# A four-layer graph network on one Trainium2 core: in the third layer, both context halves and the scores in one block of matmuls, output tiles together, a fourth context operand, the next group's norm first

## What is computed

```python
q, k, v = proj(Wq, bq), proj(Wk, bk), proj(Wv, bv)       # (b, 8, 64, 64) each
scores = einsum('bhqd,bhkd->bhqk', q, k) * SCALE * (adj + adj)
ctx = einsum('bhqk,bhkd->bhqd', softmax(scores), v)      # then heads side by side
x = x + einsum('bse,fe->bsf', ctx, Wo) + bo
```

## Time and profile before

| | us |
|---|---|
| median of 3 runs | 2230.99 (2229.94 to 2233.07) |
| profiled execution, its own time | 2231.61 |
| its span, first to last instruction | 2229.8 |
| TensorE busy | 2209.3 (99%) |
| DVE busy | 1366.5 (61%) |
| ACT busy | 778.8 (35%) |
| POOL busy | 740.7 (33%) |

### The profile page before, as it was taken

One profiled execution on the slowest core, in us unless ns is written; L12 is line 12 of the kernel. 1 busy time (PEld: TensorE's weight loads), 2 busy tenths in 40 slices (PEclk: granted clock), 3 DMA queues, 4 the chain that ended last, 5 costly groups with the idle time before them and its releaser, 6 DMA issues.

```text
span 2229.8 us, 39209 instructions
## 1 busy us (share of the span) xinstructions
PE 2209.3 (99%) x15756; PEld 1759.4 (79%) x15756; DVE 1366.5 (61%) x2712; ACT 778.8 (35%) x1393; POOL 740.7 (33%) x926
## 2 busy tenths in 40 slices
PE   8999999999999999999999999999999999999999
PEld 5788888888888887888888888888877777777776
DVE  4576666666666676555556454556787575757552
ACT  3433333333323333333232333323444343434342
POOL 1443433334433423233332223333353131313130
PEclk9999999999999999999999999999999999999999
DMA  6333333333333244322332332333453323333321
GB/s 211 76 81 105 90 102 83 88 94 87 91 92 108 83 135 133 105 81 81 91 109 83 106 98 81 85 93 104 138 160 112 100 91 99 94 95 97 92 62 38
DMA packets 142006, 220.52 MB, mean 99 GB/s; under 512 B 33920, under 2 KB 40064, under 8 KB 141824
## 3 DMA queue, kind: packets, MB, share of 16 engines
q1 hardware_dynamic: 135680, 209.62, 32.5%
q10 hardware_dynamic: 6144, 8.40, 1.6%
HBM read 84.71 MB, written 50.37 MB: 61 GB/s over the span
## 4 chain that ended last, share of the span: by engine, by line
PE 97%; DVE 1%; DMA 1%; SPq 0%; issue 0%; POOL 0%; ACT 0%; DVEq 0%; ACTq 0%; POOLq 0%
PE bank L319 54%; PE bank L309 32%; PE bank L335 3%; PE bank L555 3%; PE bank L490 2%; PE bank L460 1%; PE bank L356 1%; PE bank L299 1%; DVE yt L935 1%; PE bank L541 0%; DMA wq<-in_L_gnn_Wq_w 0%; DMA mcolt<-in_nodemask_cols 0%; SPq L957 0%; DVE hs L632 0%; DVE x L788 0%
## 5 line engine op out<-in xcount | busy, mean ns | idle before, releaser
L319 PE MATMUL bank<-w_hi,h3T_hi 128*128 128x512 f32 x768 | 305.6, 398 | 0.0
L319 PE MATMUL bank<-w_lo,h3T_hi 128*128 128x512 f32 x768 | 299.4, 390 | 0.0
L319 PE MATMUL bank<-w_hi,h3T_lo 128*128 128x512 f32 x768 | 299.1, 389 | 0.0
L964 ACT ACTIVATE Z<-bank 64x512 f32<-64x512 f32 x256 | 152.0, 594 | 319.0 <-PE bank L319 246.7
L319 PEld LDWEIGHTS bank<-w_hi,h3T_hi 128*128 128x128 f32 x768 | 144.1, 188 | 55.1 <-issue 26.0
L978 ACT ACTIVATE hn<-x,stA 128x512 f32<-128x512 f32 x192 | 140.8, 805 | 108.3 <-POOL stA L1224 108.3
L319 PEld LDWEIGHTS bank<-w_hi,h3T_lo 128*128 128x128 f32 x768 | 144.2, 188 | 30.4
L319 PEld LDWEIGHTS bank<-w_lo,h3T_hi 128*128 128x128 f32 x768 | 144.2, 188 | 29.0
L1219 POOL TENSOR_SCALAR stA<-stA 128x4 f32<-128x4 f32 x48 | 12.6, 264 | 426.6 <-DVE stA L609 426.5
L632 DVE STREAM_TRANSPOSE hs<-hn 128x512 f32<-128x512 f32 x192 | 123.8, 688 | 38.7 <-ACT hn L978 38.7
L920 DVE TENSOR_TENSOR yt<-bank,bsumt 128x512 f32<-128x512 f32 x64 | 43.9, 685 | 162.9 <-PE bank L555 162.9
(11 more groups left out here) (201 smaller groups left out, 5894.2 us busy)
## 6 DMA issues: line engine op xcount, KB each, us to landing
hGA<-hs SPq DMA_DIRECT2D x760, 64.0 KB, 2.0
mid<-x SPq DMA_DIRECT2D x32, 1024.0 KB, 4.5
x<-mid SPq DMA_DIRECT2D x32, 1024.0 KB, 5.7
x<-in_x SPq DMA_DIRECT2D x16, 1024.0 KB, 6.3
hGB<-hs SPq DMA_DIRECT2D x256, 64.0 KB, 2.0
out<-x SPq DMA_DIRECT2D x15, 1024.0 KB, 4.6
PT<-hs SPq DMA_DIRECT2D x120, 64.0 KB, 2.0
PT<-hs ACTq DMA_DIRECT2D x120, 64.0 KB, 2.1
```

Of the source, the lines that this page charges most:

```text
L319: ins = eng.matmul(b[:], h[l][:, k, ts], W[r][:, k, :], start=(k == 0 and i == 0), stop=(last and k == 3 and i == 2))
L964: return eng.activation(dst, src, ACT.Copy)
```

## The change

In every turn from 1 to 15 TensorE does both halves of the context behind the k projection, with the scores right behind them, and then the output tiles in one row. ACT normalizes the next group's tiles between the evictions of q and k, and copies both context halves behind k. DVE takes statistics and transposes of the next group first, then both context halves, then all four masks and maxima (`l2_masked`), with the output additions between these and the sums (`l2_sums`). In turn 15 the products for layer 3, and then layer 3's transposes, stand in front of the context's lo parts. There are four context operands up to group 13 and three for the last two (`ct_of`); `ct_before` names the tile that used an operand last, and ACT waits for it copy by copy instead of ahead of the pair. SP waits for output tile (13, 3) before it loads arow.

```diff
--- before.py
+++ after.py
@@ -210,8 +210,15 @@
         bv2, bo2 = abf[:].rearrange("p g t n -> p (g t n)"), blk[:, 0:512]
         zt = [alloc(pb, f"zt{i}", [128, 512]) for i in range(4)]
         PT = alloc(pb, "PT", [128, 4, 16, 32])
-        cT = [pair(pb, f"cT{i}", 4, 128) for i in range(3)]
+        cT = [pair(pb, f"cT{i}", 4, 128) for i in range(4)]
         pb.close()
+
+
+        ct_of = {(g, t): t if g < NG - 2 else (4 * g + t - 4 * NG + 8) % 3 for g in range(NG) for t in range(4)}
+        ct_before, ct_last = {}, {}
+        for at in sorted(ct_of):
+            ct_before[at] = ct_last.get(ct_of[at])
+            ct_last[ct_of[at]] = at
 
 
         pc = ExitStack()
@@ -497,7 +504,7 @@
             def l2_out(g, t):
                 pe.wait_ge(v_ct, 8 * g + 4 * (t // 2) + 4)
                 pe.wait_ge(v_wlo, lo_dve["o2"])
-                gemm(("o2", g, t), cT[(4 * g + t) % 3], 0, Wo2, (v_x3, 4 * g + t + 1))
+                gemm(("o2", g, t), cT[ct_of[g, t]], 0, Wo2, (v_x3, 4 * g + t + 1))
 
             for g in range(NG + 1):
                 on, prev = g < NG, g >= 1
@@ -505,24 +512,18 @@
                     l01_pv(NG - 1)
                 if on and g:
                     l2_gemm_T("q2", g, Wq2, a_q)
-                if prev:
-                    l2_ctx(g - 1, 0)
                 if on:
                     l2_gemm_T("k2", g, Wk2, a_k)
-                if on and prev:
-                    l2_out(g - 1, 0)
-                    l2_ctx(g - 1, 1)
-                elif prev:
-                    l2_ctx(g - 1, 1)
-                    l2_out(g - 2, 3)
-                    l2_out(g - 1, 0)
                 if prev:
-                    l2_out(g - 1, 1)
+                    for u in range(2):
+                        l2_ctx(g - 1, u)
                 if on:
                     for u in range(2):
                         l2_scores(g, u)
+                if g == NG:
+                    l2_out(g - 2, 3)
                 if prev:
-                    for t in (2,) if g == NG - 1 else (2, 3):
+                    for t in range(3 if g == NG - 1 else 4):
                         l2_out(g - 1, t)
                 if on:
                     pe.wait_ge(v_wlo, lo_dve["v2"])
@@ -778,7 +779,7 @@
                     bv = bank.of(("ctx", g, u, a))[:].rearrange("p (x m n) -> p x m n", x=2, m=4)
                     dve.wait_ge(a_ct, 8 * g + 4 * u + 2 * a + 2)
                     for x_ in range(2):
-                        ct = cT[(4 * g + 2 * u + x_) % 3]
+                        ct = cT[ct_of[g, 2 * u + x_]]
                         lo_split(ct["lo"][:, :, h], bv[:, x_], ct["hi"][:, :, h]).then_inc(v_ct, 1)
 
             def l2_out(g, t):
@@ -787,7 +788,7 @@
                 dve.wait_ge(p_xb, 4 * g + t + 1)
                 eng.tensor_tensor(xt, bank.of(("o2", g, t))[:], xt, ALU.add).then_inc(v_x3, 1)
 
-            def l2_softmax(g, u):
+            def l2_masked(g, u):
                 dve.wait_ge(*adj_loaded(2, g))
                 for r in range(2 * u, 2 * u + 2):
                     z = zt[r]
@@ -799,6 +800,8 @@
                     dve.wait_ge(v_z2, 4 * g + r + 1)
                     dve.wait_ge(p_pn, 4 * (g - 1) + r + 1 if g else 0)
                     eng.tensor_reduce(sm[r][:, 0:8], z[:].rearrange("p (s n) -> p s n", s=8), AX, ALU.max).then_inc(v_mx, 1)
+
+            def l2_sums(g, u):
                 for r in range(2 * u, 2 * u + 2):
                     dve.wait_ge(a_e2, 4 * g + r + 1)
                     m = dve.step(eng.tensor_reduce(sm[r][:, 8:16], zt[r][:].rearrange("p (s n) -> p s n", s=8), AX, ALU.add))
@@ -831,15 +834,14 @@
                     split_in_place(Wv2, "v2")
                 if g == 1:
                     split_in_place(Wo2, "o2")
-                if g == NG - 1:
-                    stats_A(3, 0)
-                if prev:
-                    l2_ctx(g - 1, 0)
-                else:
+                if g == 0:
                     l01_x2(NG - 1)
                     features2_lo(1)
-                if g == NG - 1:
-                    transposes(3, 0)
+                elif g < NG - 1:
+                    stats_A(*after2(g))
+                    transposes(*after2(g))
+                elif g == NG - 1:
+                    stats_A(3, 0)
                     dve.wait_ge(d_vec3, 64)
                     for h in range(2):
                         for k in range(4):
@@ -852,6 +854,9 @@
                     m = dve.step(eng.scalar_tensor_tensor(sc3[:], sc3[:], 1.0, bvb[:], ALU.mult, ALU.mult, accum_out=cst))
                     dve.wait_ge(s_dve, m)
                     eng.tensor_tensor(cst, cst, abc, ALU.add).then_inc(v_cst, 1)
+                    transposes(3, 0)
+                if prev:
+                    l2_ctx(g - 1, 0)
                 if g == NG:
                     l2_out(g - 2, 3)
                     l3_sums(dve, eng, 0, (1,))
@@ -866,19 +871,19 @@
                     l2_out(g - 1, 3)
                     l3_alpha(0)
                     break
-                if 0 < g < NG - 1:
-                    stats_A(*after2(g))
-                if prev:
-                    l2_out(g - 1, 0)
-                if on and 0 < g < NG - 1:
-                    transposes(*after2(g))
                 if prev:
                     l2_ctx(g - 1, 1)
                 for u in range(2):
-                    if prev:
-                        for t in ((1,), (2,) if g == NG - 1 else (2, 3))[u]:
-                            l2_out(g - 1, t)
-                    l2_softmax(g, u)
+                    l2_masked(g, u)
+                if prev:
+                    l2_out(g - 1, 0)
+                    l2_out(g - 1, 1)
+                l2_sums(g, 0)
+                if prev:
+                    l2_out(g - 1, 2)
+                l2_sums(g, 1)
+                if 0 < g < NG - 1:
+                    l2_out(g - 1, 3)
                 dve.wait_ge(d_bv2, 16)
                 for t in range(4):
                     if t == 1 and g + 1 < NG:
@@ -1092,15 +1097,14 @@
 
 
             def l2_ctx(g, u):
-                for x_ in range(2):
-                    i = 4 * g + 2 * u + x_ - 3
-                    if i >= 0:
-                        act.wait_ge(*bank.done(("o2", i // 4, i % 4)))
                 for a, h in enumerate(HALF):
                     act.wait_ge(*bank.done(("ctx", g, u, a)))
                     bv = bank.of(("ctx", g, u, a))[:].rearrange("p (x m n) -> p x m n", x=2, m=4)
                     for x_ in range(2):
-                        copy(cT[(4 * g + 2 * u + x_) % 3]["hi"][:, :, h], bv[:, x_]).then_inc(a_ct, 1)
+                        t = 2 * u + x_
+                        if ct_before[g, t]:
+                            act.wait_ge(*bank.done(("o2",) + ct_before[g, t]))
+                        copy(cT[ct_of[g, t]]["hi"][:, :, h], bv[:, x_]).then_inc(a_ct, 1)
 
             def l2_exp(g, u):
                 for r in range(2 * u, 2 * u + 2):
@@ -1119,16 +1123,13 @@
                     features2_hi(2, 1, hT2[1])
                 if on and g:
                     l2_evict("q2", g, QQ, 0, a_q)
-                if prev:
-                    l2_ctx(g - 1, 0)
-                if g == NG - 1:
-                    norm_A(3, 0)
+                if on and g:
+                    norm_A(*after2(g))
                 if on:
                     l2_evict("k2", g, KK, 4, a_k)
-                if on and 0 < g < NG - 1:
-                    norm_A(*after2(g))
                 if prev:
-                    l2_ctx(g - 1, 1)
+                    for u in range(2):
+                        l2_ctx(g - 1, u)
                 if g == NG - 1:
                     act.wait_ge(v_cst, 1)
                     act.wait_ge(*bank.done(("v2", NG - 2, 3)))
@@ -1539,6 +1540,7 @@
                     for b in range(4):
                         eng.dma_start(ar_dr.rearrange("(m b r) -> b m r", m=8, b=4)[b], rowsT[b * 32 + 8:b * 32 + 16, :]).then_inc(d_ac, 16)
                     sp.wait_ge(d_ac, 64)
+                    sp.wait_ge(*bank.done(("o2", NG - 3, 3)))
                     eng.dma_start(arow[:].rearrange("p h d -> p (h d)"), ar_dr.partition_broadcast(128)).then_inc(d_ar, 16)
                 if g == 0:
                     sp.wait_ge(v_x2, 12 * NG)
```

## The result

The kernel after takes 2248.32 us (median of 4 runs, 2247.47 to 2249.48) against 2231.85 for the kernel before in the same comparison: a ratio of 1.0077, 95% interval 1.0065 to 1.0088. I had predicted 2226.0, faster, within 2221 to 2232. Direction, size and range are wrong.

The account below looks back on a forecast made before the run. TensorE, busy 99% of the span, was taken as the bound. Terms: -11.3 (merging) + 2.0 + 4.0 (group 15 waits) = -5.3 us, giving 2226.3 against the profiled execution, 2225.7 against the median; predicted 2226.0, range 2221 to 2232.

Parts of the forecast that it names:

- Merging the blocks: Groups 1 to 15 on TensorE: one block of 256 records saves 0.75 us a group, 11.3 us in all.
- The boundary inside the block: Context to scores in the merged block: rival that it costs as much as a return, 0.39 us a group: 2232; chance 0.07.
- The matmuls themselves are the same in number and shape: TensorE's merged blocks: the matmul work is unchanged, so no term was added for it.
- I find no wait of TensorE in groups 1 to 14: Ordinary groups: everything TensorE needs from other engines is ready in time, so waits cost nothing.
- The slower rival: DVE's context subtractions: first output tile waits 1.0 us in each of 14 groups: 2240; chance 0.08.
- Statistics, norm, transposes, KK, gather: Ordinary groups: this moved work on ACT, DVE and SP is ready in time and costs nothing.
- Group 15, 2.0 us at tile (14, 0): Group 15's first output tile: TensorE waits 2.0 us for DVE's subtractions, behind attention vector products and layer-3 transposes.
- Group 15, 4.0 us behind W3's splits: Group 15's context behind the transposes: TensorE waits 4.0 us for ACT's copies to PT, between 2 and 6.
- The clock, called a rival at 0.20: Group 15's waits: TensorE's clock falls there, adding 1 to 3 us: 2228; chance 0.20.

Follow-up runs that it names:

- 192-record kernel without stops: Kernel after with half of the score products left out (block of 192 records) and group 0's score matmuls issued twice: 2226.63 us.
- the 256 scores: Kernel before with every score matmul issued twice, a block of 256 score records in each of 16 groups: 2289.87 us.
- with 192: Kernel before with only the first half of the scores issued twice, a block of 192 records: 2256.98 us.
- the kernel with the PT copies first: Kernel after with ACT's W3 splits moved behind the first context half of group 15, so the copies to PT come first: 2248.37 us.

## Why the prediction was wrong

- **Merging the blocks, 0.75 us a group: right.** In the 192-record kernel without stops a group takes 980.31 - 932.69 = 47.62 us, with a block up to 0.1 us shorter than the full one; I had said 47.6 to 47.7. The boundary inside the block costs nothing that shows; that rival falls.
- **"The matmuls themselves are the same in number and shape", and so "I find no wait of TensorE in groups 1 to 14": this is the step that failed.** The sum has no term for the supply of instructions. I listed what each matmul needs from other engines and took the instructions themselves as given. In each group TensorE stops once; from start to start around the stop 1.32 us in the mean of 14 groups, against 0.79 saved. 47.62 + 1.32 = 48.94 of the measured 49.04; the last 0.1 is the 2.07 against 1.96 us of the scores (above), about half with the stop and half with the products left out.
- **The slower rival** had the right size (1.0 us in each of 14 groups) and the wrong place. DVE's lo parts, 0.6 us to spare, were late nowhere but once, by 0.2 us, in the kernel without stops.
- **Statistics, norm, transposes, KK, gather: right**, none shows in the list of waits.
- **Group 15, 2.0 us at tile (14, 0): wrong.** The loads of the attention vector landed sooner: the products began at 1586.37, 14.8 us into the group where I had 16.0, and the block was 0.95 us late itself. Without stops the wait is 0.2.
- **Group 15, 4.0 us behind W3's splits: right in mechanism; the size, 3.7 us and 4.6 without stops, is partly luck.** The second matrix took 9.40 us to land, not 7.4, and behind its landing stood only its own four splits (2.19 us), not all eight (4.26), since ACT split the first matrix before.
- **The clock, called a rival at 0.20: it fell** in the profiled execution, 6.8 us at half speed; the 60 large matmuls behind took 15.30 us instead of 13.74, 1.6 us, and the context block of group 15, its stop taken out, 2.9 instead of 2.07. The context block was stopped too, 1.3.

Sum against the kernel before: stops 14 x 1.32 = +18.5, the 0.1 us a group +1.4, merging -11.1, turn 15 +8.2, Tother -0.4, q(1) +0.2. Without the stops the forecast would have stood: 2226.6 to 2228.1 by the estimate from the shifted kernel, against 2226.0.

Left open: why the stops differ in size from one program to the next, and what sets the start of a packet. That turn 15 in the old order gave back 4.5 us and not 8.2 is explained for the profiled execution alone, by longer stops and the clock.

## What to carry to other kernels

Where one engine is busy all the time, look at its instruction stream as an input like any other: count instructions per microsecond in the densest stretch, and look for "issue" in the list of waits; the kernel before had one, behind group 0's block (below), which I passed over. Keep blocks of small matmuls to one packet (here 128 matmuls and their weight loads), with large ones between them (group 0's block shows that even 128 can stop), and put work between a projection and whoever needs its last tile. A version with merged blocks must be judged at more than one alignment of the code: 64 small matmuls here moved 13 us (2239.69 to 2226.63).

## What was not expected of the hardware

- TensorE's instructions come in 16 KB packets of 256, one at a time as they are used: 115, 123, 131 and 139 packets for 14732, 15756, 16780 and 17804 matmuls. Where two packet edges fall within a block of small matmuls, the engine mostly stops, for 0.2 to 3.6 us; it did not in the groups 6, 8 and 10 of the 256 scores and from group 5 on with 192. In group 0, with its 128 records at one alignment for all kernels, it already stopped before, 7 large matmuls behind the block:

```profile
871.62 1.81 PE bank L319 x7
873.43 2.01 issue
```

  The Trainium skill (Runtime: NRT & Kernel Launch, "Instruction fetch mechanics") describes these 16 KiB blocks of 256 instructions and calls the cost of an edge "mostly hidden". Among large matmuls the runs agree (this stop and the one behind the 256 scores of group 12 follow right on small ones); in small ones they don't, and there the measurement decides.
- Leaving out the 64x64 products with s = 1 saves next to no time: 1.85 us for the 64 records left against 2.02 for 128.
- The clock fell behind stops of 1.8 us (0.57 over 4 us), not only behind the wait of 3.7. It did not always: in the kernel with the PT copies first stops of 2.1 and 1.8 us left it at 1.00.
